# Shared PSUM rooms for short parts of the row maxima, one room per step, and fewer running sums on GpSimd, in a two-layer gated attention and expert kernel

## The reference, cut to what matters

```python
# layer 0: causal self attention plus cross attention, added before the output projection
att  = einsum('bhqd,bhkd->bhqk', q, k) * scale;  att = where(causal, att, -inf)
y    = einsum('bhqk,bhkd->bhqd', softmax(att), v)
y    = y + einsum('bhqk,bhkd->bhqd', softmax(einsum(qc, kc) * scale), vc)
x    = x + tanh(g_xattn[0]) * (y @ Wp + bp)
x    = x + tanh(g_ffn[0]) * experts(layernorm(x))     # 8 experts, 256 tokens each
# layer 1: cross attention alone, then experts with 512 tokens each
x    = x + tanh(g_xattn[1]) * cross_attention(layernorm(x), ctx)
x    = x + tanh(g_ffn[1]) * experts(x)
```

## Time and profile before

| | us |
|---|---|
| median of 3 runs | 4285.14 |
| lowest and highest | 4281.23, 4292.8 |
| profiled execution | 4297.94 |
| its span in the trace | 4296.3 |
| TensorE busy in the span | 3806.6 (89%) |
| VectorE, ScalarE, GpSimd busy | 2547.8, 2019.5, 1795.2 |
| mean granted clock | 0.918 |

### The profile page before, as it was taken

How to read it: one execution, slowest core, us unless ns; L and a number is a source line. 1 busy time by engine, 2 the same in 40 slices (tenths; PEclk the granted TensorE clock), 3 DMA queues, 4 the chain that set the end, 5 groups by cost and what they waited for, 6 DMA issues and landing times. The chain is left out here.

```text
span 4296.3 us, 77223 instructions
## 1 busy us (share of the span) xinstructions
PE 3806.6 (89%) x30668; PEld 2654.1 (62%) x30668; DVE 2547.8 (59%) x3210; ACT 2019.5 (47%) x3511; POOL 1795.2 (42%) x878
## 2 busy tenths in 40 slices
PE   7989599999999998738997599999998739999997
PEld 5768355655655564427996455555554428888886
DVE  4345677777777774465664577777773464433342
ACT  2222265665666665006663266666664014443342
POOL 0000377777777777001110178888886000111110
PEclk9999699999999999759998799999999759999999
DMA  4478514423332430406663622222211323433331
GB/s 166 165 250 293 140 55 98 102 69 97 92 96 69 98 87 23 173 26 230 208 211 98 186 69 80 80 76 79 77 45 38 137 82 108 127 115 111 118 106 36
DMA packets 287914, 485.13 MB, mean 113 GB/s; under 512 B 22288, under 2 KB 117520, under 8 KB 285584
## 3 DMA queue, kind: packets, MB, share of 16 engines
q1 hardware_dynamic: 272016, 443.00, 33.9%
q0 software_dynamic: 14080, 37.76, 3.7%
q10 hardware_dynamic: 1536, 0.40, 0.0%
HBM read 350.67 MB, written 130.02 MB: 112 GB/s over the span
## 5 line engine op out<-in xcount | busy, mean ns | idle before, releaser
L833 DVE TENSOR_REDUCE attn_parts<-attn_mx 128x4 f32<-128x2048 f32 x540 | 1236.9, 2291 | 468.6 <-PE attn_mx L675 464.6
L789 ACT ACTIVATE attn_probs<-attn_low 128x512 f32<-128x512 f32 (+1 forms) x2368 | 1238.4, 595 | 553.4 <-PE attn_low L701 421.8
L656 POOL TENSOR_TENSOR attn_psums<-attn_psums,attn_probs 128x1024 f32<-128x1024 f32 x560 | 1330.7, 2376 | 84.9 <-ACT attn_probs L789 17.5
L701 PE MATMUL attn_low<-attn_queries,attn_keys 97*128 97x256 f32 (+1 forms) x4736 | 941.0, 318 | 22.5 <-DMA attn_queries<-attn_topT 16.5
L701 PEld LDWEIGHTS attn_low<-attn_queries,attn_keys 97*128 97x128 f32 x4736 | 680.2, 196 | 396.1 <-issue 200.5
L718 PE MATMUL attn_low<-attn_probs,attn_values 128*32 128x256 f32 x9472 | 657.1, 397 | 1.4 <-ACT attn_probs L789 1.4
L1451 DVE TENSOR_TENSOR ffn_wL<-ffn_raw,ffn_wH 128x2048 fp32r<-128x2048 f32 x128 | 293.5, 2293 | 223.4 <-ACT ffn_wH L1406 223.4
L1406 ACT ACTIVATE ffn_wH<-ffn_raw 128x2048 fp32r<-128x2048 f32 x128 | 245.3, 1916 | 338.3 <-DMA ffn_raw<-in_L_ffn_W_dram 177.4
L675 PE MATMUL attn_mx<-attn_keysn,attn_queriesn 32*128 32x512 f32 (+3 forms) x2400 | 311.9, 508 | 89.9 <-DVE attn_parts L833 45.7
L653 POOL TENSOR_TENSOR attn_psums<-attn_probs 128x1024 f32<-128x1024 f32 x88 | 209.5, 2380 | 424.9 <-ACT attn_probs L789 424.9
L718 PEld LDWEIGHTS attn_low<-attn_probs,attn_values 128*32 128x32 f32 x9472 | 253.2, 112 | 193.8 <-issue 20.9
(11 more groups left out here) (196 smaller groups left out, 4462.9 us busy)
## 6 DMA issues: line engine op xcount, KB each, us to landing
ffn_raw<-in_L_ffn_W_dram SPq DMA_DIRECT2D x128, 1024.0 KB, 5.5
attn_keys<-l_cross_keys SPq DMA_DIRECT2D x96, 512.0 KB, 5.5
attn_queries<-l_queries SPq DMA_DIRECT2D x48, 512.0 KB, 4.6
l_cross_keys<-projc_high SPq DMA_DIRECT2D x64, 256.0 KB
l_cross_keys<-projc_lowp SPq DMA_DIRECT2D x64, 256.0 KB
l_cross_values<-projc_vout SPq DMA_DIRECT2D x64, 256.0 KB
attn_keysn<-l_cross_keys SPq DMA_DIRECT2D x16, 1024.0 KB, 5.1
attn_values<-l_cross_values SPq DMA_DIRECT2D x32, 512.0 KB, 6.0
```

The source lines that it names most:

```text
L656: pool.tensor_tensor(ps, ps, at, ALU.add).then_inc(added, 1)
L701: mm = pe.matmul(out[:, n0:], KS[b][0:3 * HD + 1, h, kb * P:(kb + 1) * P], QS[b][0:3 * HD + 1, h, job.qb * QB + n0:(job.qb + 1) * QB], sta ...
L789: act.activation(probs[:, m % RING, i // 2, heads, n0:], sc[:, item % SC, :].rearrange("p (h q) -> p h q", q=QB)[:, :, n0:], ACT.Exp, scal ...
L833: dve.tensor_reduce(parts[j % ROWS_DEEP][:, :, t, part], room[:, :, 0:cols], AX.X, ALU.max).then_inc(max_read, 1)
```

## The change

- `Job`: in causal jobs qb = 0 and qb = 2 the parts shorter than 512 columns (128 for the first tile, 256 for the second) become one group that shares a room: each head's bank holds 128 columns at 0 and 256 at 128. A group is now a tuple of parts, each with its place `at`. Self units have 10 groups in place of 12.
- `Plan`: the lead-in takes as many groups as are needed for one group per step to do from then on: 11 in both attention phases. Attention 0 then has 336 groups, 11 in the lead-in, one in each of 325 steps, none in the last 11. Attention 1 has 11, then one in each of 245 steps, none in the last 11.
- Lead-in: each of the first jobs' maxima is turned between the groups (`lead_turn`), not after all of them; a group in `low` then also waits for ScalarE's copy of the turns before it. ScalarE sends each row as soon as its copy is made. TensorE waits for the reads of the `low` room only before the first scores.
- VectorE's masked operation writes its elementwise output back over the room in PSUM; `fenced` is gone, and so is its wait for the operation before.
- GpSimd: `pooled` of causal jobs keeps blocks 0, 1 and the even ones. Job qb = 2 adds blocks 0, 1, 2 (not 3), job qb = 3 blocks 0, 1, 2, 4 (not 3, 5): three additions fewer in each of eight self units, and 24 blocks more on L725.

```diff
@@ Job
+        tails = []
...
+                if unit.causal and cols < BLK and qb % 2 == 0:
+                    tails.append((t, part, cols, True, sum(x[2] for x in tails)))
+                else:
+                    self.groups.append(((t, part, cols, unit.causal and part == self.parts - 1, 0),))
+        if tails:
+            self.groups.append(tuple(tails))
...
-        self.pooled = whole if unit.causal else [kb for kb in whole[:-3] if kb < 4 or kb == 7 or kb % 2 == 0]
+        if unit.causal:
+            self.pooled = [kb for kb in whole if kb < 2 or kb % 2 == 0]
...
@@ Plan
-        while done < len(due) and due[done] <= 0:
+        lead = max(g - x for g, x in enumerate(due[:24]))
+        while done < lead:
...
-            cols = 0
-            while done < len(due) and self.free(done, m):
-                j, g = self.groups[done]
-                cols += self.jobs[j].groups[g][2]
-                if need <= len(self.groups_at[m]) > 0 and cols > BLK:
-                    break
+            while done < len(due) and self.free(done, m) and len(self.groups_at[m]) < max(need, 1):
...
@@ attention, TensorE
+        lead_turn = {j: min(plan.groups_before[j + 1] + 1, LEADS) for j in plan.turn_at[-1]}
...
+                    if room is low and turned_before(k):
+                        pe.wait_ge(exped, turned_before(k))
+                    for t, part, cols, masked, at in job.groups[g]:
...
+                    if j in plan.turn_at[-1] and lead_turn[j] // 2:
+                        pe.wait_ge(max_read, lead_turn[j] // 2 * 2)
...
                 for k in plan.groups_at[-1]:
                     maxima(k)
-                pe.wait_ge(max_read, LEADS)
-                for j in plan.turn_at[-1]:
-                    turn(j)
+                    for j in plan.turn_at[-1]:
+                        if lead_turn[j] == k + 1:
+                            turn(j)
+                pe.wait_ge(max_read, LEADS // 2 * 2)
@@ attention, VectorE
-                        if k:
-                            dve.wait_ge(max_read, k)
...
-                            op = dve.tensor_tensor_reduce(fenced[:, h, 0:cols], room[:, h, 0:cols], fence[:, BLK - cols:],
+                                op = dve.tensor_tensor_reduce(seen[:, h, :], seen[:, h, :], fence[:, BLK - cols:], 1.0, LOW,
```

More of the change, by code:

```diff
@@ L412, in __init__ @@
                 cols = min(BLK, n - part * BLK)
-                self.groups.append((t, part, cols, unit.causal and part == self.parts - 1))
+                if unit.causal and cols < BLK and qb % 2 == 0:
[4 more added lines that the diff above has]
+            self.groups.append(tuple(tails))
         whole = [kb for kb, n0, masked in self.blocks if not masked]
-        self.pooled = whole if unit.causal else [kb for kb in whole[:-3] if kb < 4 or kb == 7 or kb % 2 == 0]
+        if unit.causal:
+            self.pooled = [kb for kb in whole if kb < 2 or kb % 2 == 0]
+        else:
+            self.pooled = [kb for kb in whole[:-3] if kb < 4 or kb == 7 or kb % 2 == 0]
     def adds(self, step=None):
@@ L662, in maxima @@
                     j, g = plan.groups[k]
-                    job, (t, part, cols, masked) = jobs[j], jobs[j].groups[g]
-                    b = job.u % BUFS
+                    job, b = jobs[j], jobs[j].u % BUFS
                     if job.qb == 0 and g == 0:
@@ L671, in maxima @@
                         pe.wait_ge(max_read, k)
[L672 to L676, removed]
+                    if room is low and turned_before(k):
+                        pe.wait_ge(exped, turned_before(k))
+                    for t, part, cols, masked, at in job.groups[g]:
+                        q0 = (job.qb * (QB // P) + t) * P
+                        for h in range(GH):
+                            rows_h = slice(h * HD, (h + 1) * HD)
+                            mm = pe.matmul(room[:, h, at:at + cols], QN[b][rows_h, q0:q0 + P],
+                                           KN[b][rows_h, part * BLK:part * BLK + cols], start=True, stop=True)
                     mm.then_inc(max_ready, 1)
@@ L820, in reduce @@
                     j, g = plan.groups[k]
-                    t, part, cols, masked = jobs[j].groups[g]
                     dve.wait_ge(max_ready, k + 1)
                     room = low if k < LEADS and k % 2 else mx
-                    if masked:
-                        if k:
-                            dve.wait_ge(max_read, k)
-                        for h in range(GH):
-                            op = dve.tensor_tensor_reduce(fenced[:, h, 0:cols], room[:, h, 0:cols], fence[:, BLK - cols:],
[L829 to L834, removed]
+                    for t, part, cols, masked, at in jobs[j].groups[g]:
+                        seen = room[:, :, at:at + cols]
+                        into = parts[j % ROWS_DEEP][:, :, t, part]
+                        if masked:
+                            for h in range(GH):
+                                op = dve.tensor_tensor_reduce(seen[:, h, :], seen[:, h, :], fence[:, BLK - cols:], 1.0, LOW,
+                                                              ALU.add, ALU.max, into[:, h:h + 1])
+                        else:
+                            op = dve.tensor_reduce(into, seen, AX.X, ALU.max)
+                    op.then_inc(max_read, 1)
                     if g == len(jobs[j].groups) - 1:
```

3 lines of the change are left out of this document (2 added, 1 removed).

## The result

| | before | after |
|---|---|---|
| median (four executions each), us | 4286.98 | 4183.55 |
| profiled execution, us | 4297.94 | 4189.89 |
| granted clock, mean | 0.918 | 0.935 |

The ratio is 0.9758 with a 95% interval of 0.9735 to 0.978: 103.4 us less by the medians, 108.05 by the profiled executions, where 117 were forecast (4168, range 4145 to 4214).

The account below looks back on a forecast made before the run. TensorE was taken as the bound of both attentions, with short waits and the low clock after them. The terms, -26.5 - 12.2 + 9 - 58 - 21 - 12, gave -120.7 us; the median was put at 4168 us, range 4145 to 4214.

Parts of the forecast that it names:

- One group per step: Attention 0 from 540 us on: TensorE's waits in both kinds of double step go, 26.5 us.
- The clock: Attention 0 from 540 us on: 143 us at the lower level, 40% lost; all 58 us come back.
- GpSimd: Ends of self units in attention 0: seven waits of 1.74 us for GpSimd go, 12.2 us.
- The cost of a block of ones: Attention 0: 24 blocks no longer added on GpSimd cost TensorE 0.33 us each, 7.9 us; bound 14.6, taken as 9.
- Starts: Beginnings of both attentions: fewer double steps and a longer lead-in save 21 us in attention 0, 12 in attention 1.
- VectorE's write at nothing: Masked operations writing back into PSUM: cost taken as nothing, with an upper bound of 36 us.
- The first rival: VectorE becomes the bound in steps with a masked group: about 45 us lost, 4213 us; chance 0.18.
- Turns two steps ahead at nothing: Turns now two steps before their job, 29 more of them in attention 0: no cost.
- The last rival: Row's DMA late at 29 jobs whose turn moved to two steps ahead: 197 us slower, 4365 us; chance 0.04.
- Clock not due to waits: Second rival: only waits go, attention 0's clock stays at 0.94; 58 us and some 10 stay, 4236; chance 0.07.

Follow-up runs that it names:

- e2: Changed kernel without the shared room, the short parts being groups of their own again: 4239.42 us, ratio 0.9876 to the kernel before.
- e1: Changed kernel with GpSimd's old list back, all blocks of a self job added there: 4185.13 us, ratio 0.9741 to the kernel before.
- e4: Kernel before the change with only GpSimd's new, shorter list added: 4261.01 us, ratio 0.9912 to the kernel before.
- e9: Changed kernel without the shared room and with GpSimd's old list back: 4251.0 us, ratio 0.9914 to the kernel before.
- e5: Changed kernel with each job's turn one step earlier: 4183.58 us, ratio 0.9758 to the kernel before.
- e8: Changed kernel with the masked operation's elementwise output in SBUF again, and its wait for the operation before: 4177.94 us, ratio 0.9742 to the kernel before.
- e11: Changed kernel with all turns of the lead-in at its end, as before: 4182.75 us, ratio 0.9755 to the kernel before.
- e3: Changed kernel with eight rooms in the lead-in in place of eleven, in both attentions: 4198.46 us, ratio 0.9773 to the kernel before.
- e7: Changed kernel with turns as late as one step ahead of the job where they stood two ahead: 4435.95 us, ratio 1.035 to the kernel before.

## Why the prediction was right

- **One group per step: right.** No second wait for maxima is left; e2 brings fourteen back at 2.40 us each.
- **The clock: right in total.** Low time went from 140 to 3.5 us, 55 us at 40% against 58. With 38.7 us of waits gone, less 9 of ones, 3.5 of waits at scores and 4 behind the masked groups, that is 77; 83.3 were measured and 87.7 forecast, and the 6 between 77 and 83.3 stay open. The Trainium skill's one half (TensorE: Matmul & The Clock Gate, Terms) would make 68 us of the 55 and the sum 90, so the measured 83.3 lies between the two prices.
- **GpSimd: the step that failed inside a right sum.** I booked 12.2 us of waits and their share of the clock to it. On the changed kernel it gives nothing (e1): GpSimd's waits are 6.3 us there and the loads' 6.5, with one dip of 3.5 us, and the ones cost as much; on the kernel before it gives 38 us (e4). The other parts together give 0.9741, as much as all. The parts are not additive: e4 alone takes 85 us of low time away, and the other parts alone (e1) all but 3.5 of 140. Two parts that cure the same dips are the one reason; that in the changed plan a wait for loads comes ahead of GpSimd's and shortens it is another (e9), and why the loads come late there was not tested. The cost of a block of ones was 0.43 us (steps 3.16 and 3.58 apart), 10.3 for 24; 9 were taken.
- **Starts: right in size, not in reason.** 17.8 and 9.6 us against 21 and 12. Scores began at 474.60, 473 forecast; the first unit's last sum was at 520.89, 516 forecast. The change's own profile had bad luck: 26.8 us of low time after 470, where e5 and e8 had 13 to 14 and needed 69.3 and 69.4 us for this stretch, not 74.4. Attention 1's scores came 6.7 us behind the turn, 7 forecast, and that is luck: I took this time for the row's, but it ends with the landing of the values, in both kernels. From these scores to step 4's group it took 19.9 us, where I had 16.4: the low clock lasted through the four steps before it. The row of attention 0 did hold the scores up before, among loads, but taking it off the path brought little, since the longer lead-in and VectorE then set the scores (e11). The gain of attention 1 is from the double steps that went: with three of them back (e3) 8.5 of its 9.6 us are lost. In attention 0 the time from first scores to the first unit's last sum is 66.9 us before, 54.2 in e3 and 46.3 after; two double steps and GpSimd's wait of 1.72 us went between the first two, and no run takes them apart.
- **VectorE's write at nothing:** 4 us on the path (e8), inside the bounds of 0 and 36. The first rival's 45 us don't follow from its own terms: 18 us of waits and 14 dips of 4 us at 40% are 40.
- **Turns two steps ahead at nothing:** right, with 0.4 us to spare for a row, and 3.7 us of waits at the four jobs where that was too little. The last rival's mechanism is real (e7, 254 us) and begins one step later.
- **Clock not due to waits:** refuted for the kernel before by e4 (140 to 55 us of low time) and for the changed one by e2 (3.5 to 68).

The forecast's 15.6 us excess come from 4 in the steps, 6 in the two starts, 3 elsewhere, and 3 from the medians: the forecast put the median after 9 us under the profile's time, and it was 6.3 under it.

## What to carry to other kernels

Where TensorE is the bound, count a wait with the low clock behind it, and try the edits one at a time on top of the others: two that cure the same dips are worth the dips once. A wait that costs no more than the work that removes it, here GpSimd's against the ones, is not worth moving work for. Before calling a transfer late, list all transfers that the waiting instruction needs, with their landings, and time the one in question where nothing else loads the queues.

## What the runs showed of the hardware that was not expected

- The same wait of 1.75 us was followed by a mean granted clock of 0.74 over 20 us in one run (e9) and by 1.00 in another (e1), and two waits of 0.5 to 1.1 us some 4 us apart by no dip at any of the six unit ends of e1 and three of e9 that had them.
- A VectorE operation that reads PSUM and writes it back took 35 to 42 ns longer than with its output in SBUF (723 against 688 ns at 512 columns, 322 against 280 at 128), and the next one could start that much later.
- The same small row took 9.7 us from the first turn to the scores with the DMA engines 0.96 busy (kernel before, attention 0) and 3.8 us with them 0.01 busy (e11). The last load of the values took 26.0 us from issue to landing at the start of attention 1, and 10.1 us at 643.8 us in e1.
